# Attention denominators: reciprocals spread over features by TensorE instead of through DRAM

## What is computed

```python
xn = layernorm(x)
q, k, v = split(xn @ w_qkv);  q = elu(q) + 1;  k = elu(k) + 1
running_kv, running_ksum = decay_scan(k * v), decay_scan(k)
den = clip(sum(q * running_ksum, over the 16 features of a head), 1e-6, None)
out = q * running_kv / den          # den: one value per head and token
x + out @ w_out + moe(xn)
```

## Time and profile before

| | us |
|---|---|
| median of 3 runs | 133.48 (133.03 to 133.86) |
| profiled execution, its own time | 132.86 |
| span of the profiled execution, first to last instruction | 131.2 |
| TensorE clock granted, mean | 0.993 of full speed |

### The profile page before, as it was taken

How to read it: one execution, slowest core, us unless ns; L and a number is a source line. 1 busy time by engine, 2 the same in 40 slices (tenths; PEclk the granted TensorE clock), 3 DMA queues, 4 the chain that set the end, 5 groups by cost and what they waited for, 6 DMA issues and landing times.

```text
span 131.2 us, 2388 instructions
## 1 busy us (share of the span) xinstructions
PE 124.0 (94%) x830; PEld 107.5 (82%) x830; DVE 76.2 (58%) x157; ACT 50.6 (39%) x99; POOL 31.4 (24%) x53
## 2 busy tenths in 40 slices
PE   4989999999999999999999999999999999999870
PEld 1258758787888588999998999899999989999670
DVE  0898876999999967783838333635531324023090
ACT  1675796799856445231313131372222231000000
POOL 7803000018887000101010020202020202478300
PEclk9999999999999999999999999999999999999997
DMA  3675999999942202069999999998881111033336
GB/s 102 206 253 114 315 362 226 227 356 386 387 164 80 90 0 65 20 142 311 334 409 362 370 315 322 371 347 285 303 252 40 38 57 50 9 111 106 94 125 200
DMA packets 20036, 27.25 MB, mean 208 GB/s; under 512 B 1356, under 2 KB 16884, under 8 KB 20024
## 3 DMA queue, kind: packets, MB, share of 16 engines
q1 hardware_dynamic: 14056, 21.24, 50.5%
q0 software_dynamic: 1344, 3.43, 8.2%
q10 hardware_dynamic: 4624, 2.43, 6.6%
HBM read 19.90 MB, written 7.19 MB: 206 GB/s over the span
## 4 chain that ended last, share of the span: by engine, by line
PE 86%; DMA 6%; issue 2%; DVE 2%; POOL 1%; ACT 0%; SPq 0%; DVEq 0%; POOLq 0%
PE ps L1042 21%; PE ps L286 10%; PE ps L285 10%; PE ps L287 10%; PE ps L1056 9%; DMA gu<-in_L_ffn_w_gate_up_dram 6%; PE ps L911 5%; PE ps L986 4%; PE ps L917 4%; PE ps L924 4%; PE ps L980 3%; PE ps L972 2%; PE ps L857 1%; DVE x_sb L840 1%; PE ps L963 1%
## 5 line engine op out<-in xcount | busy, mean ns | idle before, releaser
L1042 PE MATMUL ps<-xgT,gu 128*128 128x144 f32 x256 | 34.2, 287 | 0.6 <-DMA gu<-in_L_ffn_w_gate_up_dram 0.6
L1042 PEld LDWEIGHTS ps<-xgT,gu 128*128 128x128 f32 x256 | 32.3, 190 | 1.2 <-issue 1.0
L794 DVE TENSOR_TENSOR wqkv<-rz,ps 128x288 f32<-128x288 f32 x16 | 7.3, 454 | 26.4 <-ACT rz L545 26.3
L418 POOL DMA_DIRECT2D sorted_rows<-yrow x9 | 6.3, 697 | 60.5 <-DVE yrow L789 55.8
L1056 PE MATMUL ps<-wqkv,dn 128*128 128x144 f32 x128 | 17.4, 289 | 0.0
L545 ACT ACTIVATE rz<-ps 128x288 f32<-128x288 f32 x16 | 6.6, 410 | 26.5 <-PE ps L1042 26.5
L1056 PEld LDWEIGHTS ps<-wqkv,dn 128*128 128x128 f32 x128 | 16.1, 190 | 0.0
L410 POOL DMA_INDIRECT sorted_rows<-xn,slot_row x8 | 11.2, 1397 | 19.2 <-ACT xn L483 17.7
L285 PE MATMUL ps<-xT_hi,sgu_hi 128*128 128x512 f32 x32 | 13.0, 405 | 0.0
L287 PE MATMUL ps<-xT_hi,sgu_lo 128*128 128x512 f32 x32 | 12.5, 391 | 0.0
L286 PE MATMUL ps<-xT_lo,sgu_hi 128*128 128x512 f32 x32 | 12.5, 390 | 0.0
(11 more groups left out here) (146 smaller groups left out, 217.8 us busy)
## 6 DMA issues: line engine op xcount, KB each, us to landing
gu<-in_L_ffn_w_gate_up_dram SPq DMA_DIRECT2D x8, 1024.0 KB, 6.1
dn<-in_L_ffn_w_down_dram SPq DMA_DIRECT2D x8, 512.0 KB
sorted_rows<-zeros SPq DMA_DIRECT2D x1, 2592.0 KB, 16.7
wqkv<-sorted_rows SPq DMA_DIRECT2D x10, 144.0 KB
sorted_rows<-yrow POOLq DMA_DIRECT2D x9, 144.0 KB, 4.0
sgu<-_ffn_shared_gate_up_dram SPq DMA_DIRECT2D x1, 1024.0 KB, 6.1
rden_rows<-rden ACTq DMA_DIRECT2D x1, 1024.0 KB, 14.0
ksum<-rden_rows ACTq DMA_DIRECT2D x2, 512.0 KB, 8.1
```

The costliest lines, as they stand in the source:

```text
L794: V.tensor_tensor(hr[:, 2 * h:2 * h + 2, :].rearrange("p f s -> p (f s)"), act_sb[:, h, 0:2 * SLOTS], ps[:, 2 * h + 1, 0:2 * SLOTS], ALU.m ...
L1042: ins = mm(ps[:, 2 * h + u, (f % 2) * SLOTS:(f % 2 + 1) * SLOTS], gu[p][:, kc, col:col + P], xgT[:, kc, :], start=(kc == 0), stop=(kc == K ...
```

## The change

The reciprocals no longer go through DRAM. `head_of` becomes 128 wide (16 copies of the 8 head columns), so that each strip of bank 6 holds each denominator four times. One more transpose behind `head_sums` gives `head_row`, the transposed `head_of` (bank 7, copied by ACT). DVE clips `den_h` [128, 512] and takes the reciprocals in four parts of 128 columns, one in each of four gaps between tiles. The first 8 rows of each strip become the high part of the reciprocal and the next 8 the low part (`rden_hi` by ACT, `rden_split` by DVE, with the masks `high_row`, `low_row` built at the start). Behind the loop, four products with 16 rows of contraction, one in each 32-row strip, spread them over 128 features into banks 0, 1, 4 and 5: three ahead of `shared_tile(7, 0)`, one between `shared_tile(7, 0)` and `shared_tile(7, 1)`. The multiplication with `q * kvsum`, the rounding and the subtraction move from the loop to behind it, in blocks of 512 columns. The additions at the end are put in another order.

```diff
-            sp.wait_ge(s_denc, 1)
-            for g in range(NH * KC):
-                sp.dma_start(den_rows...[g // KC, g % KC], den_h[g * STRIP:g * STRIP + HC, :]...).then_inc(s_denst, 16)
...
+                    act.wait_ge(s_hrow, 1)
+                    A(head_row[:, :], ps[:, HROW, 0:P], ACT.Copy).then_inc(s_hrowc, 1)
...
             hidden_hi(LAST - 1)
-            act.wait_ge(s_denst, 16 * NH * KC)
-            act.dma_start(den[:, :], den_rows).then_inc(s_denld, 16)
             expert_tile(0)
-            act.wait_ge(s_rden, 1)
-            act.dma_start(rden_rows..., rden[:, :].unsqueeze(1).broadcast_to([NT * HEADS, HD, P])).then_inc(s_rdram, 16)
             expert_tile(1)
             expert_tile(2)
-            act.wait_ge(s_rdram, 16)
-            for c in range(KC):
-                act.dma_start(rspread[:, c, :]..., rden_rows...[c]).then_inc(s_spread, 16)
             expert_tile(3)
             expert_tile(4)
-            for c in range(KC):
-                act.wait_ge(s_att, c + 1)
-                A(att_hi[:, c, :], kvsum[:, c, :], ACT.Copy).then_inc(s_atth, 1)
+            act.wait_ge(s_rden, 4)
+            A(rden_hi, rden, ACT.Identity, scale=high_row[:, 0:1]).then_inc(s_rhigh, 1)
...
+            attention_hi(0)
             gate_silu(LAST)
+            attention_hi(1)
+            attention_hi(2)
             hidden_hi(LAST)
+            attention_hi(3)
...
+            def attention(g):
+                dve.wait_ge(s_spread, g + 1)
+                dve.wait_ge(s_qkv_sum, KC)
+                V.tensor_tensor(kvsum[:, c, cols], kvsum[:, c, cols], ps[:, spread_bank[g], :], ALU.mult).then_inc(s_att, 1)
...
+            link(V.tensor_scalar(den_h, den_h, EPS_DEN, None, ALU.max))
+            head_reciprocals(0)
             kv_scan(2)
             first_tile(1)
             kv_scan(3)
+            head_reciprocals(1)
...
+            attention(0)
             rows_copy(total, 0, 16 * (E // 2))
+            attention(1)
+            attention(2)
             hidden(LAST)
+            attention(3)
             hidden_lo(LAST)
+            for g in range(NH * KC):
+                attention_lo(g)
...
+            for i in range(TH + 1):
+                rows_add(i)
+            for i in range(NT):
+                dense_add(i)
+                if 0 < i < TH:
+                    rows_add(i + TH)
...
+                tr(ps[:, HROW, 0:P], head_of[:, :, :]..., ident[:, :]).then_inc(s_hrow, 1)
...
+            def spread_reciprocals(gs):
+                pe.wait_ge(s_rsplit, 1)
+                pe.wait_ge(s_hrowc, 1)
+                for g in gs:
+                    rows = slice(g * STRIP, g * STRIP + 2 * HC)
+                    mm(ps[:, spread_bank[g], :], head_row[rows, :], rden_split[rows, :], start=True, stop=True).then_inc(s_spread, 1)
...
+            pe.wait_ge(s_silu, 2 * total)
+            pe.wait_ge(s_hr, 2 * total)
+            pe.wait_ge(s_xgc, total + 1)
+            spread_reciprocals(range(NH * KC - 1))
             shared_tile(LAST, 0)
+            spread_reciprocals([NH * KC - 1])
             shared_tile(LAST, 1)
...
+                if i in att_of_bank:
+                    pe.wait_ge(s_att, att_of_bank[i])
...
-            pe.wait_ge(s_attl, KC)
+            pe.wait_ge(s_attl, NH * KC)
```

More of the change, by code:

```diff
@@ L62, in build @@
         root_eps = sb("root_eps", [P, 1], F32)
-        head_of = sb("head_of", [P, STRIP], F32)
+        head_of = sb("head_of", [P, P // HC, HC], F32)
+        head_row = sb("head_row", [P, P], F32R)
+        low_row4 = sb("low_row4", [P, P // STRIP], F32)
+        low_row = sb("low_row", [P, 1], F32)
+        high_row = sb("high_row", [P, 1], F32)
         spread = sb("spread", [HEADS, KC, P], F32)
@@ L280, in build @@
         DEN = 6
+        HROW = 7
+        spread_bank = [0, 1, 4, 5]
+        att_of_bank = {0: 1, 1: 2, 4: 3, 5: 4}
+        rden_hi = att_hi[:, 0, 0:512]
+        rden_split = att_lo[:, 0, 0:512]
         bank_user = {3: 0, 4: 1, 5: 2, 6: 3}
@@ L371, in _ @@
             pool.memset(nothing[:, :], 0.0)
-            pool.memset(head_of[:, :], 1.0).then_inc(s_const, 1)
+            pool.memset(head_of[:, :, :], 1.0).then_inc(s_const, 1)
             pool.memset(spread[:, :, :], 1.0).then_inc(s_const, 1)
@@ L570, in _, with attention_hi @@
                 expert_tile(t)
+            def attention_hi(g):
+                c, cols = g % KC, slice(g // KC * 512, (g // KC + 1) * 512)
+                act.wait_ge(s_att, g + 1)
+                A(att_hi[:, c, cols], kvsum[:, c, cols], ACT.Copy).then_inc(s_atth, 1)
+            attention_hi(0)
             gate_silu(LAST)
+            attention_hi(1)
+            attention_hi(2)
             hidden_hi(LAST)
+            attention_hi(3)
         @block.vector
@@ L797, in expert_tile, with head_reciprocals, attention_lo @@
                         rows_copy(t, b, stored)
+            def head_reciprocals(part):
+                cols = slice(part * P, (part + 1) * P)
+                V.reciprocal(rden[:, cols], den_h[:, cols]).then_inc(s_rden, 1)
+            def attention(g):
+                c, cols = g % KC, slice(g // KC * 512, (g // KC + 1) * 512)
+                dve.wait_ge(s_spread, g + 1)
+                dve.wait_ge(s_qkv_sum, KC)
+                V.tensor_tensor(kvsum[:, c, cols], kvsum[:, c, cols], ps[:, spread_bank[g], :], ALU.mult).then_inc(s_att, 1)
+            def attention_lo(g):
+                c, cols = g % KC, slice(g // KC * 512, (g // KC + 1) * 512)
+                dve.wait_ge(s_spread, NH * KC)
+                dve.wait_ge(s_atth, g + 1)
+                V.tensor_tensor(att_lo[:, c, cols], kvsum[:, c, cols], att_hi[:, c, cols].bitcast(F32), ALU.subtract).then_inc(s_attl, 1)
             def first_tile(t):
@@ L802, in _ @@
             first_tile(0)
-            dve.wait_ge(s_denld, 16)
-            link(V.tensor_scalar(den[:, :], den[:, :], EPS_DEN, None, ALU.max))
-            V.reciprocal(rden[:, :], den[:, :]).then_inc(s_rden, 1)
+            dve.wait_ge(s_denc, 1)
+            link(V.tensor_scalar(den_h, den_h, EPS_DEN, None, ALU.max))
+            head_reciprocals(0)
             kv_scan(2)
```

68 lines of the change are left out of this document (34 added, 34 removed).

## The result

| | median of the runs | range | n |
|---|---|---|---|
| before | 134.19 us | 133.03 to 135.75 | 6 |
| after | 131.56 us | 131.51 to 132.12 | 6 |

The ratio is 0.9844, 95% interval [0.9811, 0.9877]: 1.6% faster. I had forecast no change (133.3). The time lies near the 131.2 that I gave for rival D, but for the most part by luck, as will be seen. The profiled execution of after took 131.59, against 132.86 of before, with a granted clock of 1.00.

A forecast was written before the change was run, and what follows sets the result against it. PE, with 124.0 us of matmuls in a 131.2 us span, was taken as the bound; 132.86 - 1.12 + 0.11 + 1.10 = 132.95 for the profiled execution, 133.57 on the median; 133.3 named between them, range 131.2 to 134.7.

The forecast's parts named there:

- rival D: End of kernel: stall goes because a few more instructions shift where it falls; 2.2 us less, 131.2 us; chance 0.2.
- stalls in tiles 3 and 5: Loop, PE waiting for late expert weights: both stalls go once the DRAM traffic is removed, -1.12 us.
- transpose of `head_of`: PE behind the head sums: one added transpose, priced from eight such transposes taking 0.87 us, +0.11 us.
- two groups of spreading products: PE behind the loop: four products in row strips, 0.55 us taken for each group, +1.10 us.
- stall in `attention_out`: End of kernel: late first DVE addition and PE gap, no wait explaining them, about 1.0 us on PE; left unchanged.
- No more than 1.12, since PE has no other wait there: Loop, late weight loads: upper bound on what removing the DRAM traffic could gain, 1.12 us.
- stalls at the loads are longer in runs without a profile: Loop loads: case within the forecast sum that could make the change faster by over 1%; given 0.05.
- rival B: First products of tiles 3 and 5: the load stalls stay, nothing is gained there, 134.7 us; chance 0.15.
- rival C: Spreading products: the strips don't overlap, 0.7 to 0.9 more than the sum, 134.2 us; chance 0.1.
- (a): Price of a spreading group read from the head sums, four products in column strips: 0.53 us.
- (b): Price of a spreading group read from the decay products, 16 rows and one column: 0.63 us with its columns.
- at no cost: Work moved on DVE and ACT, in and behind the loop, fits into gaps and delays nothing; no term.

The follow-up runs named there:

- e1: Kernel before with its three transfers of the reciprocals through DRAM cut to almost nothing, every other instruction kept; 131.90 us, ratio 0.9833 to before.
- second pair: The kernels before and after, unchanged, run once more for their traces; 134.19 us (ratio 1.0033) and 131.81 us (ratio 0.9858).
- e4: Kernel after with transfers like the removed ones put back on ACT's queue, carrying unused constants; 133.75 us, ratio 0.9969 to before.
- e2: Kernel before with 16 more instructions on PE, waits already met, ahead of the eight `shared_down` calls; 133.87 us, ratio 1.0004 to before.
- e3: Kernel before with 32 more instructions on PE, waits already met, ahead of the eight `shared_down` calls; 135.22 us, ratio 1.0107 to before.
- e15: Kernel after with a memset on POOL ahead of the gathers, meant to delay them; 131.91 us, ratio 0.9879 to before.

## Why the prediction was wrong

The terms of the sum, for the profiled execution (132.86), beside what came:

| step | predicted | measured |
|---|---|---|
| stalls in tiles 3 and 5 | -1.12 | -1.12, but -2.1 in the medians (e1) |
| transpose of `head_of` | +0.11 | +0.06 |
| two groups of spreading products | +1.10 | +1.25 on PE, but the second, 0.62, is not on the chain of the end |
| stall in `attention_out` | 0 | -1.13 on PE, nothing at the end |
| behind the last product | 0 | -0.53 |

**The step that failed** is "The change alters neither these products nor their place; I leave the stall where it is." With it the sum ran along PE to its last product and took the rest as fixed. What the sum left where it was is the wait of DVE's first addition, and the end hangs on that wait and not on PE: in both pairs of traces the first addition comes with POOL's last gather, 0.83 and 1.67 us earlier in after. So the second group of products, charged with 0.55, costs nothing in these executions. And POOL needs 14.70 us from `rows_copy` to its last gather instead of 15.14 (14.71 and 15.14 in the second pair): the last row store is issued 1.44 us behind `rows_copy` instead of 1.82 and lands 2.53 us after its issue instead of 3.51 (2.51 and 3.50 in the second pair), while the first two gathers take 0.89 more (1.49 and 1.44, for 1.05 and 0.99). What makes the store slow in before is one of its 16 increments: the 15th comes 2.52 us after the issue, against 2.45 in after, but the 16th 0.99 behind it, against 0.08. Why that is so, and why these gathers are slower, I can't say; in e1, without the traffic, the store isn't quicker (3.63). "No wait in the program explains it" was right, but the trace had the hint: the last gather landed at 124.27, the stall ended at 124.4. e4 shows the size without any reading of chains: all but the traffic is worth -0.4 us, where the sum had +1.21.

**Rival D** gave the right time, but as luck. "A few more instructions shift where it falls" is what e2 and e3 refute. Its 2.2 us were PE's 1.0, DVE's 0.4 and SP's 0.8: PE's gap went, without an effect on the end, and the wait of DVE stayed (2.94 us for 3.17). "Nothing in the program holds it there" was true; the gathers did, as far as the traces tell. (Taken from 133.3, 2.2 gives 131.1, not 131.2.)

**The second miss** is a bound. "No more than 1.12, since PE has no other wait there" takes one execution for all. The loss at late loads differs between executions, and the median of before lies above its profiled one by 0.6 in the first three runs and 1.3 over six; I had seen 0.62 and given "stalls at the loads are longer in runs without a profile" 0.05. With 2.1 for the traffic (e1) and 0.4 for the rest of the change (e4), 134.19 - 2.1 - 0.4 = 131.7, against 131.56. (The parts come from other runs than the total, and e1 and e4 leave each of them open by 0.7 us and more, so this is a plausibility and no proof.)

**Right**: the tiles at 6.6, the DMA share under or near 0.9 (0.95 at most, so my limit of 0.9 was missed in one of three windows), no wait on `gu`, so that rival B falls; the spreading products of the first group start at 104.638, 104.642 and 104.645, 4 ns apart, so that rival C falls. The Trainium skill (TensorE: Matmul & The Clock Gate, Part 3: Packing small matmuls) has row strips start some 4 ns apart; the trace agrees. **The size of the groups** was off by 0.15: I took 0.55, near the 0.53 of the head sums (a); 0.62 and 0.63 are (b), the decay products, with 0.63. Of the two rows the one with the same number of rows in the strip was the nearer, not the one with the same columns. **Nothing on PE waits** for the work of DVE and ACT behind the loop, as said: attention(0) at 105.17, `rows_copy` at 106.51, hidden(7) at 109.28, the last subtraction done by 113.8, 6.7 us ahead of its use. But "at no cost" isn't shown: POOL's first two gathers take 0.89 longer in after, and they are on the chain of the end. DVE's four subtractions (111.27 to 113.76) run at that time; that they are the cause is not shown, since the first gather of e15 took 1.05 beside two of them.

## What to carry to other kernels

When a stall in a trace has no wait in the program behind it, put beside its end whatever else ends then, on other engines and queues, before it is left in the sum as a constant. Then ask what the end of the kernel hangs on: a change on the busiest engine is worth nothing where the last stores wait for something else, and a gap that closes there is no gain. A loss from contention that one execution shows is a sample: the spread of the runs of before against those of a variant without the traffic says how large it is in the median. And price a packed matmul group as one fixed cost of entering and leaving (0.4 here) plus one product: gather all products into one group, and don't pack a single one.

## What was not expected of the hardware

- PE's semaphore increments can come 0.9 to 3.7 us late, at about the moment when the last of eight indirect gathers on POOL's software queue begins to report its landing, while PE goes on computing; in 13 of 20 traces, not in all, on chips and at times that I can't tell apart. The mechanism is open.
- 2 MB of traffic beside the expert weights costs 0.9 to 1.7 us at the loads in nine executions and 2.1 in the median of the runs [1.2 to 3.3], and the time of the kernel spreads over 1.5 to 2.0 us instead of 0.4 to 0.6.
- Of a row store in 16 parts, 15 report within 2.52 us of the issue and the last one 0.99 later; the kernel with the change has the same store without that straggler (2.45, 0.08).
- Products in row strips of 16 rows: 0.62 to 0.63 us for one, three or four of them together (512 columns); over all 128 rows 0.23 each.
- Waits on PE that are already met cost nothing between the products of `shared_down`: 11.52 us with 32 such instructions among them, 11.51 without.
